# Two attention layers rebuilt as one pipeline each: paired 48-row scores, projection between steps

## What is computed

```python
# a0
q, k, v = (x @ qkv_w.T).reshape(B, N, 3, H, D).transpose(2, 0, 3, 1, 4)
q = q * cos + _rotate_half(q) * sin
k = k * cos + _rotate_half(k) * sin
attn = jnp.einsum('bhqd,bhkd->bhqk', q, k) * SCALE
diff = jnp.where(pos[None, :] - pos[:, None] > 0, 0.0, pos[None, :] - pos[:, None])
attn = attn + (diff[None, :, :] * slopes[:, None, None] * MAX_BIAS)[None]
out = jnp.einsum('bhqk,bhkd->bhqd', softmax(attn), v)
x = layernorm(x + out.transpose(0, 2, 1, 3).reshape(B, N, C) @ proj_w.T + proj_b)
# a3: the same with another rotation, without the position term and the output bias
```

## Time and profile before

| | us |
|---|---|
| median of 3 runs | 2179.75 |
| lowest and highest | 2179.23, 2183.18 |
| the profiled execution's own time | 2180.4 |
| its span in the profile | 2178.6 |
| first stage (a0), up to the next block | 383.9 |
| a3, from its layernorm to the next block | 1510.4 to 1839.3 |

### The profile page before, as it was taken

The page is one execution under the profiler, slowest core; times in us unless marked ns, Lnnn a source line. Parts: engine busy times, 40 slices in busy tenths (PEclk is TensorE's granted clock), DMA queues, the critical chain, the costliest instruction groups (busy, mean ns, idle before and its releaser), DMA issues. The chain is left out here.

```text
span 2178.6 us, 25289 instructions
## 1 busy us (share of the span) xinstructions
PE 1634.6 (75%) x8319; PEld 714.7 (33%) x8319; DVE 1139.2 (52%) x2326; ACT 872.1 (40%) x1220; POOL 390.0 (18%) x249
## 2 busy tenths in 40 slices
PE   4399998899659887577997500652489997779997
PEld 2044444333213332332343200651223322334443
DVE  7777772100039999254775392222588882533332
ACT  3155555422368874211666200111135655234333
POOL 4200000000059985000222005023400000000000
PEclk8599999899769999698999755785679998889998
DMA  3411110100000000001103400125501111000000
GB/s 106 97 22 26 22 22 1 53 0 0 21 4 5 4 4 0 26 0 31 40 21 137 184 0 6 31 34 50 145 15 24 30 23 56 36 5 0 0 0 19
DMA packets 52176, 70.90 MB, mean 33 GB/s; under 512 B 11172, under 2 KB 46092, under 8 KB 50204
## 3 DMA queue, kind: packets, MB, share of 16 engines
q1 hardware_dynamic: 50044, 67.36, 10.7%
q0 software_dynamic: 2048, 2.48, 1.7%
HBM read 47.81 MB, written 18.35 MB: 30 GB/s over the span
## 5 line engine op out<-in xcount | busy, mean ns | idle before, releaser
L614 ACT ACTIVATE a_probs_sb<-a_t_ps 128x1024 f32<-128x1024 f32 x256 | 262.2, 1024 | 283.3 <-PE a_t_ps L551 156.8
L530 PE MATMUL a_s_ps<-a_ks,a_qs 96*128 96x512 bf16 x512 | 213.2, 418 | 86.8 <-PEq L70 53.6
L648 DVE CUSTOM_DVE_ANT_0 a_biased<-a_s_ps,a_bias 128x512 f32<-128x512 f32 x256 | 169.1, 686 | 77.2 <-issue 67.1
L652 DVE TENSOR_REDUCE a_least_sb<-a_s_ps 128x1 f32<-128x512 f32 x256 | 167.8, 687 | 60.7 <-PE a_s_ps L530 59.4
L547 PE MATMUL a_t_ps<-a_qs,a_ks 126*128 126x512 bf16 (+1 forms) x512 | 195.1, 386 | 0.0
L1252 DVE TENSOR_TENSOR_SCAN s_h<-s_dA,s_dbu 128x1024 f32<-128x1024 f32 x64 | 146.6, 2290 | 52.1 <-POOL s_dbu L1217 44.3
L566 PE MATMUL a_o_ps<-a_probs_sb,a_vpad 128*32 128x256 f32 x2048 | 163.2, 391 | 4.7 <-ACT a_values_sb L622 2.1
L1217 POOL TENSOR_TENSOR s_dbu<-s_du,s_bs 128x1024 f32<-128x1024 f32 x64 | 152.3, 2391 | 27.8 <-DVE s_h L1252 27.3
L2576 DVE TENSOR_TENSOR c_gated_sb<-c_hid,c_g_ps 128x2048 f32<-128x2048 f32 x32 | 73.2, 2287 | 144.9 <-ACT c_hid L2566 144.9
L2566 ACT ACTIVATE c_hid<-c_up_ps,c_b 128x512 f32<-128x512 f32 x128 | 88.0, 687 | 142.1 <-PE c_up_ps L2535 142.1
L530 PEld LDWEIGHTS a_s_ps<-a_ks,a_qs 96*128 96x128 bf16 x512 | 49.9, 98 | 224.2 <-issue 70.7
(11 more groups left out here) (422 smaller groups left out, 2621.5 us busy)
## 6 DMA issues: line engine op xcount, KB each, us to landing
x_wu<-in_x_wu SPq DMA_DIRECT2D x2, 4096.0 KB, 16.9
a_stacks<-a_p SPq DMA_DIRECT2D x16, 384.0 KB, 3.7
a_qs<-a_stacks SPq DMA_DIRECT2D x32, 192.0 KB, 3.5
a_ks<-a_stacks SPq DMA_DIRECT2D x32, 192.0 KB, 3.9
a_stacks<-a_p SPq DMA_DIRECT2D x16, 256.0 KB, 3.3
q_q<-q_q SPq DMA_DIRECT2D x32, 128.0 KB, 2.3
x_wd<-in_x_wd SPq DMA_DIRECT2D x2, 2048.0 KB, 32.1
c_w<-in_c_w SPq DMA_DIRECT2D x2, 2048.0 KB, 10.4
```

The lines of the kernel that those rows point to most:

```text
L530: nc.tensor.matmul(s_ps[n % 2][:, :], qs[0:LEAST_AT, h, t * P:(t + 1) * P], ks[0:LEAST_AT, h, :], start=True, stop=True).then_inc(scores_r ...
L614: nc.scalar.activation(probs[:, j % 4, :, :], t_ps[j % 2][:, :, :], ACT.Exp, scale=-1.0).then_inc(probs_ready, 1)
L648: nc.vector.tensor_tensor_reduce(out=biased[:, n % 2, :], in0=src, in1=bias[:, h, at:at + N], scale=1.0, scalar=3.0e38, op0=ALU.add, op1=A ...
L652: nc.vector.tensor_reduce(least[:, g % 2, n:n + 1], src, axis=AX.X, op=ALU.min).then_inc(least_ready, 1)
```

## The change

`project_and_split` goes. `attend` is one block whose loop over `x`, 160 steps in Python with nothing left of engine loops, does everything. A step is one pair of heads and one tile of queries; a group has 8 steps, a batch 32.

- The two heads of a pair stand in one tile `stack`, the first from row 0, the second from row 64, 48 rows each, with the three rows for the least scores behind them (51). The zeroed rows and their memsets go. `scores(x)` issues both heads' matmuls into two of now four banks `s_ps`; DVE takes the least of both: two operations in a0, one of 1024 columns in a3.
- `turned(y, e)` with y = x - LAG (12 in a0, 13 in a3; it was 16 pairs) is a 51-row matmul a head. In a0 the distance between tiles is a matmul of its own over 9 rows, `alibi_k` and `alibi_q`, for the columns of later tiles alone (384, 256, 128 or none), and the three `slopes_diag` matmuls stay. `t_ps` has two banks instead of four, one per head of the pair, and ACT takes one exponential of 512 columns for each.
- `sum_values` runs on every second step over all 512 queries, between the two heads' turned scores.
- One bank, `spare`, takes in turn the turned least scores, the next batch's four projections (steps 5 to 8) and values (step 28), the tail's transposes (18 to 21, 23) and its projection (26). ACT copies the turned least scores out (`keep_least`), POOL splits them.
- Only batch 0 is projected before the first step. Its bf16 parts are cut by ACT and DVE, those of later batches by ACT at steps 10 and 13 and POOL. SP stores and loads the stacks of the next batch between the placing DMAs. POOL makes `slopes_diag`.
- The last batch's tail turns all four tiles into the four score banks at once.

```diff
-STACK = HD * len(Q_PARTS)
+SLICES = len(Q_PARTS)
+STACK = HD * SLICES
 GROUP = 4
 GROUPS = HEADS // GROUP
+ALL_GROUPS = B * GROUPS
+HEAD_PAIRS = HEADS // 2
 VPAD = 32
-LEAST_AT = 96
 LEAST_ROWS = 3
-PAIRS_OF_TILES = QT - 1
-LOWER_ROWS = LEAST_ROWS + 9 * PAIRS_OF_TILES
+HALF_AT = 64
+ALIBI_ROWS = 9
...
+GROUP_STEPS = GROUP // 2 * QT
+BATCH_STEPS = GROUP_STEPS * GROUPS
+ATT_STEPS = BATCH_STEPS * B
+U = 2 * GROUP_STEPS
+PROB_RING = 6
+SUM_LAG = 3
...
+    LAG = 12 if alibi else 13
...
+    def spare_steps(i):
+        steps = [9, 17, 25] if i < B else []
+        if i > 0:
+            steps += [1, 23, 26]
+        if 0 < i < B:
+            steps += [18, 19, 20, 21]
+        if i + 1 < B:
+            steps += [5, 6, 7, 8, 28]
+        return sorted(steps)
+
...
+            def load(k):
+                i, g = divmod(k, GROUPS)
+                if g == 0 or i == 0:
+                    wait(sp, stored, 16 * 6 * (i + 1))
+                wait(sp, turned_ready, U * (k - GROUPS + 1))
+                source = stacks_dram[i].rearrange("a (w e d) s t -> a e (d s) w t", e=2, d=HD)
+                for a in range(2):
+                    for e in range(2):
+                        sp.dma_start(stack[rows(e, STACK), a, places(k), :],
+                                     source[a, e, :, 2 * g:2 * g + 2, :]).then_inc(loaded[g], 16)
+
+            def place(k):
+                wait(sp, least_split, k + 1)
+                for r in range(LEAST_ROWS):
+                    both = slice(STACK + r, HALF_AT + STACK + r + 1, HALF_AT)
+                    sp.dma_start(stack[both, 0, places(k), :].rearrange("e w (t p) -> e (w t) p", p=P),
+                                 least_parts[:, k % 2, r, :]).then_inc(least_placed[k % 2], 16)
...
+            def scores(x):
+                k, u = divmod(x, GROUP_STEPS)
+                pair, t = divmod(u, QT)
+                place = 2 * (k % GROUPS) + pair
+                if u == 0:
+                    wait(pe, loaded[k % GROUPS], 16 * 4 * (k // GROUPS + 1))
+                if x == 0:
+                    wait(pe, products, 4)
+                wait(pe, least_ready, x - 1)
+                for e in range(2):
+                    last = nc.tensor.matmul(s_ps[:, 2 * (x % 2) + e, :],
+                                            stack[rows(e, STACK), 0, place, t * P:(t + 1) * P],
+                                            stack[rows(e, STACK), 1, place, :], start=True, stop=True)
+                last.then_inc(scores_ready, 1)
+
...
+            def turned(y, e):
+                k, u = divmod(y, GROUP_STEPS)
+                t, pair = divmod(u, 2)
+                place = 2 * (k % GROUPS) + pair
+                h = GROUP * (k % GROUPS) + 2 * pair + e
+                if y == 0 and e == 0:
+                    wait(pe, minus_placed, 32)
+                if u == 0 and e == 0:
+                    wait(pe, least_placed[k % 2], 16 * LEAST_ROWS * (k // 2 + 1))
+                wait(pe, probs_ready, 2 * y + e - 1)
+                last = nc.tensor.matmul(t_ps[:, e, :], stack[rows(e, STACK + LEAST_ROWS), 1, place, t * P:(t + 1) * P],
+                                        stack[rows(e, STACK + LEAST_ROWS), 0, place, :], start=True, stop=not alibi)
+                if alibi:
+                    if y == 0 and e == 0:
+                        wait(pe, tables_ready, 2)
+                        wait(pe, diag_ready, 3)
+                    if t < QT - 1:
+                        nc.tensor.matmul(t_ps[:, e, (t + 1) * P:], alibi_k[rows(e, ALIBI_ROWS), h // 2, :],
+                                         alibi_q[rows(e, ALIBI_ROWS), h // 2, 0:N - (t + 1) * P],
+                                         start=False, stop=False)
+                    for r in range(3):
+                        last = nc.tensor.matmul(t_ps[:, e, t * P:(t + 1) * P], slopes_diag[:, r, h, :],
+                                                steps_table[:, :], start=False, stop=(r == 2))
+                last.then_inc(turned_ready, 1)
...
+            def sum_values(z):
+                k, t = divmod(z, KT)
+                i, g = divmod(k, GROUPS)
+                wait(pe, probs_ready, 4 * z + 4)
+                if t == 0:
+                    wait(pe, values_kept, k)
+                    if g == 0:
+                        wait(pe, v_kept, i + 1)
+                for h in range(GROUP):
+                    y = 2 * z + h // 2
+                    last = nc.tensor.matmul(o_ps[h * VPAD:(h + 1) * VPAD, :], vpad[:, i % 2, t, g * GROUP + h, :],
+                                            probs[:, y % PROB_RING, h % 2, :], start=(t == 0), stop=(t == KT - 1))
+                last.then_inc(sums_ready, 1)
...
+            for x in range(TOTAL):
+                i, s = divmod(x, BATCH_STEPS)
+                y = x - LAG
+                z = y - SUM_LAG
+                if x < ATT_STEPS:
+                    scores(x)
+                if 0 <= y < ATT_STEPS:
+                    turned(y, 0)
+                if 0 <= z < ATT_STEPS and z % 2 == 1:
+                    sum_values(z // 2)
+                if 0 <= y < ATT_STEPS:
+                    turned(y, 1)
+                if i == B and s == 18:
+                    wait(pe, least_ready, ATT_STEPS)
+                    wait(pe, values_kept, GROUPS * B)
+                    for t in range(QT):
+                        turn_values(B - 1, t, s_ps[:, t, :]).then_inc(last_turned, 1)
+                spare_uses(i, s)
...
+            def keep_least(i, s):
+                k = turn_group(i, s)
+                wait(act, spare_written, spare_use(i, s) + 1)
+                wait(act, least_split, k - 1)
+                nc.scalar.activation(least_turned[:, k % 2, :], spare[0:U, 0:P], ACT.Copy).then_inc(turned_kept, 1)
+
+            def exps(y, e):
+                wait(act, turned_ready, 2 * y + e + 1)
+                if e == 0:
+                    wait(act, sums_ready, (y - PROB_RING) // 2 + 1)
+                nc.scalar.activation(probs[:, y % PROB_RING, e, :], t_ps[:, e, :], ACT.Exp,
+                                     scale=-1.0).then_inc(probs_ready, 1)
...
+            def least_of(x):
+                k, u = divmod(x, GROUP_STEPS)
+                pair, t = divmod(u, QT)
+                wait(dve, scores_ready, x + 1)
+                if u == 0:
+                    wait(dve, turned_kept, k - 1)
+                banks = s_ps[:, 2 * (x % 2):2 * (x % 2) + 2, :]
+                if alibi:
+                    for e in range(2):
+                        h = GROUP * (k % GROUPS) + 2 * pair + e
+                        wait(dve, bias_ready, h + 1)
+                        nc.vector.memset(spacer[:, 2 * u + e:2 * u + e + 1], 0.0)
+                        at = (QT - 1 - t) * P
+                        last = nc.vector.tensor_tensor_reduce(
+                            out=biased[:, x % 2, e, :], in0=banks[:, e, :], in1=bias[:, h, at:at + N], scale=1.0, scalar=3.0e38,
+                            op0=ALU.add, op1=ALU.min, accum_out=least[:, k % 2, e, u:u + 1])
+                    last.then_inc(least_ready, 1)
+                else:
+                    nc.vector.tensor_reduce(least[:, k % 2, :, u], banks, axis=AX.X, op=ALU.min).then_inc(least_ready, 1)
...
+                whole = least_turned[:, k % 2, :]
+
+                def then(instruction):
+                    instruction.then_inc(split_step, 1)
+                    done[0] += 1
+                    wait(pool, split_step, done[0])
+
+                wait(pool, turned_kept, k + 1)
+                wait(pool, least_placed[k % 2], 16 * LEAST_ROWS * (k // 2))
+                then(nc.gpsimd.tensor_copy(part[0], whole))
+                then(nc.gpsimd.tensor_tensor(least_rest[:, :], whole, part[0], ALU.subtract))
+                then(nc.gpsimd.tensor_copy(part[1], least_rest[:, :]))
+                nc.gpsimd.tensor_tensor(part[2], least_rest[:, :], part[1], ALU.subtract).then_inc(least_split, 1)
+```

Where instructions go, at the places of which the prediction speaks. PE in a0, one pair of heads in the full stretch of the kernel before: two units and half the queries of a value sum.

```order
L530 MATMUL a_s_ps<-a_ks,a_qs 128x512
L547 MATMUL a_t_ps<-a_qs,a_ks 128x512
L551 MATMUL a_t_ps<-a_steps,a_slopes_diag 128x128 x3
L530 MATMUL a_s_ps<-a_ks,a_qs 128x512
L547 MATMUL a_t_ps<-a_qs,a_ks 128x512
L551 MATMUL a_t_ps<-a_steps,a_slopes_diag 128x128 x3
L566 MATMUL a_o_ps<-a_probs_sb,a_vpad 32x256 x4
```

764 lines of the change are left out of this document (359 added, 405 removed).

## The result

The changed kernel takes 2251.5 us (2244.9 to 2255.8), the kernel before 2180.9 beside it: a ratio of 1.032, 95% interval 1.029 to 1.035. The change costs 71 us. The prediction was 2150.7 with a range of 2100 to 2205: the time lies outside it, and the change makes the kernel slower where a gain was forecast.

A forecast was written before the change was run, and what follows sets the result against it. PE was taken to bound a0, ACT's round trip a3. a0: 57 + 282.5 + 24 + 15 + 9.3 = 387.8, 8 us lost; a3: 1561.5 + 180 + 28 + 20 + 9.3 = 1798.8, 37 gained; forecast 2150.7 us, range 2100 to 2205.

The forecast's parts named there:

- Heads: Before the first scores: only batch 0 projected first, scores at 41 in a0 and 1546 in a3, gain 41 and 28.
- Changes of shape: PE in a0's full groups: 48 changes of row shape a group at 0.11 us each, 5.3 us a group.
- Rivals 1 and 2: Changes between row shapes in a0: at 0.20 us, 2220 us, chance 0.11; free between 64 and 32 rows, 2130, chance 0.17.
- Overlap: a0's score matmuls of the two heads, at rows 0 and 64, overlap: 8 pairs take 1.73 us.
- rival 3: The two 48-row score matmuls don't overlap: 28 us in a0, hidden in a3, 2178 us; chance 0.05.
- Placing chain: Between turning the least scores and the turned score: ACT's copy, POOL's split, SP's DMAs, 5.5 to 6.1 us.
- A wait: PE at each group's first turned score, for the small DMA: 1.0 us in a0, 1.3 in a3; 15 and 20 us.
- Rival 4: The placing chain is 1.4 us a group longer than assumed, over 31 groups: 2194 us; chance 0.07.
- A full group of a0: PE's streaming of 12.6 us plus 5.3 us of shape changes: 17.9 us a group, against 16.07 before.
- sixteen groups of 17.9: a0's loop on PE: 286 us less 4 for 12 steps without scores, 282.5 us.
- Two steps: a3's full loop, bound by ACT with its round trip to PE: 2.83 us for two steps, 1.42 a step.
- what projections, tails and copies add: Added to a3's loop: 17 us of projections and tails beyond PE's slack, 11 of ACT's copies.

The follow-up runs named there:

- lag14: The changed kernel with turned scores 14 and 15 steps behind in place of 12 and 13, in both layers: 2202.5 us, ratio 1.011.
- lag14_alibi64: The changed kernel with distance matmuls of 64 rows instead of 9 and turned scores two steps later: 2136.6 us, ratio 0.979.
- alibi32: The changed kernel with 32 rows instead of 9 in the distance matmuls, added rows zeros: 2200.4 us, ratio 1.009.

## Why the prediction was wrong

- **Heads.** 37.5 and 1544.1 against 41 and 1546: right. The first turned scores came at 60.4 and, less the 90.6, at 1565.7, 3 and 4 us later than worked out. In a0 DVE waited 0.93, 0.93 and 0.49 us for three of the four projections; most of this stretch ran at half clock.
- **Changes of shape.** Predicted 0.11 us with 0.09 to 0.20 as bounds, measured 0.09 to 0.10, also from 64 to 32 rows. Rivals 1 and 2 both fell.
- **Overlap.** L427 start in pairs, two in 0.39 us: right, rival 3 fell.
- **Placing chain.** From transpose to turned score 5.4 us around 352, predicted 5.5 to 6.1. A wait was predicted as 1.0 us and measured as 1.01 at 357.5, but for every group: 15 us were put down in a0 and 20 in a3, and 7.5 and 4.8 came. Rival 4, a longer chain, fell.
- **A full group of a0.** Predicted 17.9 without waits and additions. lag14's groups without spare work take 17.9 at the full clock. The sum was right.
- **The failed step** is the line after it: sixteen groups of 17.9. "The streaming, at 0.216 us for 512 columns" is the time at the full clock, and the prediction carried it through the whole layer because the earlier trace rows had PEclk 1.00 in the full stretch. It took the clock for a property of the stage, while the change took away what held it. a0 ended 82.7 us later than the predicted 387.8. lag14's fifteenth group took 27.5 us at half clock, and the same group of lag14_alibi64 15.7 at full with 12 changes fewer, so about 16.9 with them: 1.63 times. 214 us at half then cost 214 x (1 - 1 / 1.63) = 83 us. That is the miss, as an estimate from one pair of groups. alibi32, with the same matmuls and order, bears it out: its a0 ends at 432.4 with 121.2 us at half, and less 0.387 of these it would be 385.5, as the changed kernel's 470.5 less 83 is 387.5.
- The signs stood in rows already quoted: the scores before were matmuls of 96 rows and the turned scores of 126, in a3 of 99. The change makes them 48, 51 and 9.
- **a3** ended at 1907.5 - 90.6 = 1816.9, predicted 1798.8, 18 us late: 4 before the first turned score; 12 in the loop, which had the clock at half for 59 of 240 us; and 1.5 in the end, 10.8 against 9.3. Of the 12, some 8 or more are the clock's: the same loop in alibi32, with 35 us at half, took 232.7 us in place of 240.4, and groups that take 16.6 and 13.1 us there took 18.2 and 17.4 here. Two steps were predicted as 2.83 us, and where nothing is added the trace has 2.88 from sum to sum; from 1686.31 to 1689.68 it is 3.37, with a copy of 0.59 by ACT in it. The waits came to 4.8 us and not 20, so either what projections, tails and copies add, put at 28, was too small by up to 20 us, or the clock cost more than 8; that is not told apart.
- The two misses, 82.7 and 18.1, make the 100.8 us between 2151.4 and 2252.2. Smaller terms of a0 were off both ways: the waits 7.5 us too high, the first turned score 3 too early and the end 2 too short (11.3 from the last turned score, against 9.3). No rival of mine had this mechanism. The range reached 2205 by rows of changes and waits, and held nothing for a clock that falls.

Still open: what measure of the work the clock follows. Rows at work count (9 to 32 rows, 128 against 48), pauses count at the margin, and order counts; the runs do not say how they add up.

## What to carry to other kernels

Cutting a matmul's rows, or splitting a wide one into narrow ones, keeps its columns and looks free; but the granted clock of a stage is a result of what runs in it, so price the stage at both levels of the clock, and ask what the change takes out of the rows at work. If it falls while PE is busy, put narrow matmuls on different rows side by side and keep one shape together (one edit here, 105 us), widen the narrowest with zero rows (76 us), and take out pauses (49 us, some 12 of them the waits themselves). Where a kernel's times scatter, look at the mean clock of each run first.
